# Moving the expert-weight conversion, the row scatters and the second norm's buffer inside a cross-attention + MoE kernel

## The reference, cut to what matters

```
x = x + cross_attention(layernorm(x), ctx)     # 16 batches of 256 rows of 256; 16 heads of 64; 73 + 4 keys,
                                               # two softmaxes (73 text keys, 4 image keys), low-rank
                                               # corrections on q, k, v, o
x = x + moe(layernorm(x))                      # 8 experts, top 2, 256 -> 512 (silu) -> 256
def moe(x):
    logits = x @ gate_w
    top_w  = softmax(top2(logits))
    out    = sum over the two picks of top_w * (silu(x @ w1[e]) @ w2[e])
```

## Time and profile before

| | us |
|---|---|
| median of 3 runs (829.76 to 836.23) | 834.12 |
| the profiled execution, its own time | 830.35 |
| its span in the profile | 828.6 |
| start, up to the first scores of batch 1 | 0 to 92.85 |
| batches 1 to 14, first scores to first scores | 92.85 to 528.79 |
| batch 15 and the way to the experts | 528.79 to 592 |
| experts | 592 to 828.6 |

### The profile page before, as it was taken

How to read it: one execution, slowest core, us unless ns; L and a number is a source line. 1 busy time by engine, 2 the same in 40 slices (tenths; PEclk the granted TensorE clock), 3 DMA queues, 4 the chain that set the end, 5 groups by cost and what they waited for, 6 DMA issues and landing times.

```text
span 828.6 us, 23021 instructions
## 1 busy us (share of the span) xinstructions
PE 695.4 (84%) x7980; PEld 580.9 (70%) x7981; DVE 528.4 (64%) x1226; ACT 449.2 (54%) x772; POOL 494.1 (60%) x584
## 2 busy tenths in 40 slices
PE   6757889799788789789799898864499999999994
PEld 2235777677677677677677776643398888888894
DVE  5955786686586586586586586573255555555552
ACT  1537775674675675675674675661244343443441
POOL 2227467667667667667668668666147555655565
PEclk9999999999999999999999999987599999999998
DMA  9901001101101101101101101101535556555450
GB/s 267 285 1 40 28 18 61 52 14 64 52 13 64 52 13 64 52 13 64 52 13 65 52 13 64 53 13 62 161 66 98 81 89 98 86 91 81 83 91 6
DMA packets 41676, 54.69 MB, mean 66 GB/s; under 512 B 6320, under 2 KB 36016, under 8 KB 41648
## 3 DMA queue, kind: packets, MB, share of 16 engines
q1 hardware_dynamic: 26176, 35.90, 14.8%
q0 software_dynamic: 14384, 17.33, 12.0%
q10 hardware_dynamic: 1088, 1.08, 0.4%
HBM read 30.36 MB, written 25.76 MB: 68 GB/s over the span
## 4 chain that ended last, share of the span: by engine, by line
PE 57%; ACT 14%; issue 13%; DVE 8%; DMA 2%; POOL 2%; SPq 1%; another core or an unknown queue 1%; POOLq 1%; ACTq 0%; DVEq 0%
PE ps L1321 46%; PE ps L1382 5%; ACT pt_s L873 4%; PE ps L1392 2%; ACT wstage L992 2%; ACT xn L935 2%; PE ps L439 2%; DVE ot_s L1073 2%; DMA out_x<-pt_s,token_of 1%; POOL out_x L413 1%; PE ps L1347 1%; ACT ot_s L873 1%; DVE picked L1227 1%; DVE prob L1114 1%; ACT row_words L944 1%
## 5 line engine op out<-in xcount | busy, mean ns | idle before, releaser
L413 POOL DMA_INDIRECT out_x<-pt_s,token_of x78 | 125.9, 1615 | 31.1 <-issue 30.2
L492 ACT ACTIVATE q_s<-ps 128x512 f32<-128x512 f32 x78 | 46.6, 597 | 132.6 <-PE ps L1321 132.1
L1321 PE MATMUL ps<-q_s,ffnw 128*128 128x256 f16 x936 | 110.0, 275 | 0.0
L1321 PE MATMUL ps<-ffnw,ot_s 128*128 x936 | 108.7, 273 | 0.1
L565 DVE TENSOR_TENSOR ot_s<-q_s,ot_s 128x512 f16<-128x512 f32 x78 | 54.0, 692 | 85.8 <-ACT ot_s L496 57.8
L1144 DVE TENSOR_REDUCE mx<-prob 128x16 f32<-128x1168 f32 x64 | 47.9, 790 | 95.3 <-ACT prob L913 90.9
L1321 PEld LDWEIGHTS ps<-ffnw,ot_s 128*128 128x128 f16 x936 | 90.2, 98 | 13.3 <-issue 1.9
L1321 PE MATMUL ps<-wo_s,ot_s 128*128 128x256 f16 x768 | 93.8, 281 | 5.4 <-DVE ot_s L1073 4.4
L1321 PEld LDWEIGHTS ps<-q_s,ffnw 128*128 x936 | 90.7, 99 | 10.7 <-issue 0.2
L731 POOL TENSOR_TENSOR prob<-prob,mx 128x1168 f32<-128x1168 f32 x64 | 77.6, 1235 | 31.0 <-DVE mx L1144 30.7
L1321 PE MATMUL ps<-xt_s,wq_s 128*128 128x256 f16 x768 | 89.0, 277 | 3.8 <-DVE xt_s L1073 1.9
(11 more groups left out here) (179 smaller groups left out, 1311.9 us busy)
## 6 DMA issues: line engine op xcount, KB each, us to landing
prob<-rows_dram SPq DMA_DIRECT2D x39, 264.0 KB
wstage<-in_ffn_w SPq DMA_DIRECT2D x16, 512.0 KB
x_sb<-in_x SPq DMA_DIRECT2D x4, 1024.0 KB, 11.8
out_x<-x_sb SPq DMA_DIRECT2D x16, 256.0 KB, 2.2
out_x<-pt_s,token_of POOLq DMA_INDIRECT x78
rows_dram<-wstage ACTq DMA_DIRECT2D x4, 264.0 KB
rows_dram<-wstage SPq DMA_DIRECT2D x4, 264.0 KB
pt_s<-in_wq SPq DMA_DIRECT2D x2, 512.0 KB, 4.4
```

Source lines behind the costliest of these rows:

```text
L413: pool.indirect_dma_start(out_rows, bass.IndirectOffsetOnAxis(ap=token_of[:, j % UNROLL, c:c + 1], axis=0), y_sb[:, j % UNROLL, c, :], Non ...
L492: act.activation(h32[:, half, :], h_ps(j, half), ACT.Silu, scale=1 / WSCALE).then_inc(silu_done, 1)
L1321: last = pe.matmul(o, lhs(a, n), rhs(c, n), start=(i == 0), stop=(i == len(steps) - 1))
```

## The change

Five edits. ACT's two conversions of the expert-weight piece move from behind `row_high`, near the end of a batch, to between `xt(b+1)` and `copy_scores(b, 1)` near its start. `normalise_x(b+2)` moves from between `ot` 1 and `ot` 2 to behind `exp(b, 0)`, and drops its wait for `row_lo`, since `x2n` gets a buffer of its own (2 KB per partition). ACT's `row_high(b-1)` and `gap_e(b-1)` come behind all four `ot`. DVE calls `place_rows` behind `ot` 0 and no longer behind `ot` 1, and `slot_i` is written only when the scatters that still read it are over (a new wait for `scattered`). POOL issues the four scatters one batch later, those of batch b-2, behind `normalise(b, 1)`; behind them come the weight split, `router_gap`, the bias add, `row_low` and `weigh_picks` of b-1. PE's and SP's programs stay as they are, but for the name of the buffer.

```diff
-        x2n = xn
+        x2n = sb("x2n", [P, TPB, DM], F32)
...
-            def body(b, first, last):
+                for pick in range(TOPK):
+                    for t in range(TPB):
+                        pool.indirect_dma_start(
+                            rows_dram, bass.IndirectOffsetOnAxis(ap=slot_i[:, pick, t:t + 1], axis=0),
+                            row_words[:, t, :], None).then_inc(scattered, 16)
+
+            def body(b):
+                first, settled = isinstance(b, int) and b == 0, not (isinstance(b, int) and b < 2)
                 shift(b, 0)
                 shift(b, 1)
                 normalise(b, 0)
                 if not first:
                     rstd_2(b - 1)
                 normalise(b, 1)
+                if settled:
+                    scatter(b - 2)
+                pool.wait_ge(fw_hi, b + 1)
+                fw = [ffnw[:, part, bass.ds(b, 1), :].rearrange("p e n -> p (e n)") for part in (0, 1)]
+                pool.tensor_tensor(fw[1], wstage[:], fw[0], ALU.subtract).then_inc(fw_split, 1)
                 if not first:
-                    row_low(b - 1)
+                    router_gap(b - 1)
                 pool.wait_ge(xn_done, b + 1)
...
                 if not first:
-                    router_gap(b - 1)
-                pool.wait_ge(fw_hi, b + 1)
-                fw = [ffnw[:, part, bass.ds(b, 1), :].rearrange("p e n -> p (e n)") for part in (0, 1)]
-                pool.tensor_tensor(fw[1], wstage[:], fw[0], ALU.subtract).then_inc(fw_split, 1)
-                if not first:
+                    row_low(b - 1)
                     weigh_picks(b - 1)
-                    scatter(b - 1)
-                    scatter_pick(1)
...
+            scatter(BATCH - 2)
             pool.wait_ge(fw_split, BATCH)
...
# ACT
                 if not last:
                     xt(b + 1)
+                act.wait_ge(fw_in, 16 * b + 16)
+                act.activation(wstage[:], wstage[:], ACT.Copy, scale=WSCALE).then_inc(fw_scaled, 1)
+                act.wait_ge(fw_scaled, b + 1)
+                act.activation(ffnw[:, 0, bass.ds(b, 1), :].rearrange("p e n -> p (e n)"), wstage[:], ACT.Copy
+                               ).then_inc(fw_hi, 1)
                 copy_scores(b, 1)
                 exp(b, 0)
+                if x_left:
+                    normalise_x(b + 2)
...
                 pt(b, 7)
+                for k in range(4):
+                    ot(b, k)
                 if not first:
                     row_high(b - 1)
-                act.wait_ge(fw_in, 16 * b + 16)
-                act.activation(wstage[:], wstage[:], ACT.Copy, scale=WSCALE).then_inc(fw_scaled, 1)
-                act.wait_ge(fw_scaled, b + 1)
-                act.activation(ffnw[:, 0, bass.ds(b, 1), :].rearrange("p e n -> p (e n)"), wstage[:], ACT.Copy
-                               ).then_inc(fw_hi, 1)
-                ot(b, 0)
-                ot(b, 1)
-                if not first:
                     gap_e(b - 1)
-                if x_left:
-                    act.wait_ge(row_lo, b + 1)
-                    normalise_x(b + 2)
-                ot(b, 2)
-                ot(b, 3)
...
# DVE
+                dve.wait_ge(scattered, 64 * b + 16)
                 with nc.allow_low_precision(reason="whole numbers below 2 ** 24"):
                     dve.tensor_reduce(slot_i[:].rearrange("p k t -> p (k t)"),
...
                 ot(b, 0)
-                ot(b, 1)
                 if not first:
                     place_rows(b - 1, chain)
-                ot(b, 2)
-                ot(b, 3)
+                for k in range(1, 4):
+                    ot(b, k)
```

More of the change, by code:

```diff
@@ L782, in scatter @@
                 pool.tensor_tensor(hold_p[:, 0:1], zero8[:, 0:1], zero8[:, 1:2], ALU.add)
-                scatter_pick(0)
-            def scatter_pick(pick):
-                for t in range(TPB):
-                    pool.indirect_dma_start(
-                        rows_dram, bass.IndirectOffsetOnAxis(ap=slot_i[:, pick, t:t + 1], axis=0),
-                        row_words[:, t, :], None).then_inc(scattered, 16)
-            def body(b, first, last):
+                for pick in range(TOPK):
[5 more added lines that the diff above has]
+                first, settled = isinstance(b, int) and b == 0, not (isinstance(b, int) and b < 2)
                 shift(b, 0)
@@ L804, in body @@
                 if not first:
-                    router_gap(b - 1)
-                pool.wait_ge(fw_hi, b + 1)
-                fw = [ffnw[:, part, bass.ds(b, 1), :].rearrange("p e n -> p (e n)") for part in (0, 1)]
-                pool.tensor_tensor(fw[1], wstage[:], fw[0], ALU.subtract).then_inc(fw_split, 1)
-                if not first:
+                    row_low(b - 1)
                     weigh_picks(b - 1)
-                    scatter(b - 1)
-                    scatter_pick(1)
             pool.wait_ge(misc_in, 32)
-            body(0, True, False)
-            with pool.Fori(1, BATCH - 1) as b:
-                body(b, False, False)
-            body(BATCH - 1, False, True)
+            body(0)
+            body(1)
+            with pool.Fori(2, BATCH) as b:
+                body(b)
+            scatter(BATCH - 2)
             pool.wait_ge(fw_split, BATCH)
@@ L827, in _ @@
             rstd_2(BATCH - 1)
+            router_gap(BATCH - 1)
             row_low(BATCH - 1)
-            router_gap(BATCH - 1)
             weigh_picks(BATCH - 1)
             scatter(BATCH - 1)
-            scatter_pick(1)
             ffn_pool(pool)
```

## The result

The changed kernel takes 847.85 us (median of 4 runs, 841.72 to 852.01), the kernel before 831.94 on the same chip (827.89 to 836.23): ratio 1.0192, 95% interval 1.0141 to 1.0242. It is slower by 1.9%, where 795 was forecast. The profiled execution took 852.01, its span is 850.2 (before: 828.6).

A forecast was written before the change was run, and what follows sets the result against it. PE, the busiest engine, waits 4.2 us per batch at the scores. Gains 1.98 + 1.08 - 0.1 give 2.96 per batch, 38.5 over 13; ends +1.0 and -2.0 make 790.9, plus 3.8 gives 795 us, range 782 to 815.

The forecast's parts named there:

- 1, copies leave the end: ACT's weight conversions leave the batch's end, so the next first scores start earlier: gain 1.83 us per batch.
- Part 2: Early conversions delay ACT's second score copy: cost 0.1 us per batch, bounds nothing and 2.9 with a 6.1 us load.
- 3, scatters leave the start: The four scatters no longer meet PE's second scores, whose gaps go: gain 1.98 us per batch.
- Part 4: Scatters behind the second `normalise` stall PE around `attend` 0 and 1: cost 1.0 us per batch, between 0 and 1.9.
- Part 6: POOL's split, bias add, `row_low` and `weigh_picks` behind the scatters end near t = 3.9 of the next batch: no cost.
- The clock: A lower granted clock in more batches would spoil the sum; it was left as before, with no chance given.
- The ends: Outside the steady loop: batches 0 and 1 together cost 1.0 us, the last batch and tail gain 2.0.
- Rival 3 (held signals): The moved stall also holds back PE's signals to ACT: 1.5 to 2.3 us more per batch, 815 to 825; chance 0.10.
- The slower rival: Expert piece lands late, SP waiting for POOL's split, ACT before the second copy: 860 at 5 us later; chance 0.06.
- Part 5: On DVE, `slot_i`'s new wait for scatters is free: the last leaves POOL 3.9 us before `slot_i` is due.
- The rival that ties the stall to the loop: PE's stall in the second scores stays when the scatters move: 29.16 us per batch, 811 in all; chance 0.13.
- the 2.1: In batch 0, moving the conversions away from the batch's end gives back 2.1 us.

The follow-up runs named there:

- the first experiment: The changed kernel with the four scatters, of batch b-1 again, in a row at the end of POOL's batch behind `weigh_picks`: 862.34 us, ratio 1.0304.
- the last run above: The kernel of 767.80 with its third scatter behind the second half of `normalise` and the fourth behind the weight split: 820.86 us, ratio 0.9939.
- the mended kernel: The changed kernel with paired scatters, early weight load, bias ahead of `router_gap`, batch 0's copies late, `row_high` ahead of `ot`, `row_low` behind `weigh_picks`: 777.93 us, 0.9349.
- the kernel of 767.80: The mended kernel with its four scatters one at a time, behind each half of POOL's `shift` and `normalise`: 767.80 us, ratio 0.9225.

## Why the prediction was wrong

| part | put at, us per batch | measured |
|---|---|---|
| 1, copies leave the end | -1.83 | wait for the slots -2.26 |
| 2, copies at the new place | +0.1 | +1.05 |
| 3, scatters leave the start | -1.98 | -1.98 |
| 4, scatters at the new place | +1.0 (0 to 1.9) | +2.8 |
| 6, POOL's end of batch | 0 | +0.9 |
| lower clock in batches 2 to 14 | as before | some +0.75 |
| ends: batches 0 and 1; tail | +1.0; -2.0 | +4.4; 0 |

- **Part 4 is the step that failed.** The count was near: the first gap comes 24 + 8 + 20 = 52 pairs of weight load and matmul behind the first scatter (58 counted, one or two too many, since the projection had run for 0.30 us when the first scatter began), the last one ends 5.77 us behind it (5.76). Two things were wrong. The pairs of keys and transposes run faster than I put them, and the reserve was gone after 2.5 us (378.77 - 376.24), not 3.5, so that the stall met keys and transposes and not `attend`: PE's gaps of this kind came to 0.28 + 0.46 + 0.90 = 1.64, where I had taken 1.0 (bounds 0 to 1.9). And I had put at nothing, without a reason, what the row of four does to the other engines: ACT took up late what PE had finished, so it copied keys, `pt` and `x2t` late, and PE waited 0.82 more and started each next step later. Rival 3 (held signals) said so, and the row that should have raised its chance above 0.10 was in batch 15 of the kernel before (536.86 above). Whether PE's signal comes late or ACT's own next instruction, no run here separates; ACT is late even where PE has no gap (370.14 in the first experiment). As a rival it was priced at 1.5 to 2.3 us per batch; with part 6's loss beside it that is what came.
- **Part 2.** I put the load at t = 0.2 and its landing at 3.4. SP issues the image values first, so it went out at t = 1.06 and landed at 4.8, 3.7 later. The bound of 2.9 us held. The slower rival named the right victim, ACT in front of the second copy, but the wrong culprit: SP waited for `attend`, not for POOL's split.
- **Part 6.** I weighed POOL's end of batch for when it ends, not for what runs beside it. The bias add moved beside DVE's product of the picks. The Trainium skill ("SBUF — State Buffer", section "SBUF: two separate sides") says that an operation of DVE with two SBUF inputs and a GpSimd operation that reads SBUF exclude each other. The runs agree: 1.09 and 0.97 us beside the bias add and beside `row_low`, 0.19 beside neither.
- **Part 5** was right, and what it lacked is now known in part: a single last scatter let ACT go 4.3 us after its start. If the last of a row does so too, which is an estimate, `slot_i` is free by 384.5 (380.17 + 4.3), 3.4 us before it is written (387.90).
- **Parts 1 and 3** were right. The rival that ties the stall to the loop, and with it the rule of the Trainium skill ("Runtime: NRT & Kernel Launch", "Instruction fetch mechanics") as an explanation of this stall, is refuted: the second scores are whole at the same place of the loop (1.03 us at 361.56).
- **The ends.** In batch 0 the load went out at 77.94, t = 2.9, behind the transfers of the image values. The queries came 4.5 us later, near the 5.0 I had put, but I had put nothing for the clock: the wait of 6.02 us that this makes is followed by PE at its lower level, another 2.8 us, and the 2.1 did not come back at that batch's end. With the copies late, batch 0 takes 22.4 to 22.6 in every kernel. In the tail the last projection does start 2.6 us earlier in its batch (29.55 against 32.11 after its first scores), but POOL is at the scatters of batch 14 until 588.2 and the last norm waits for it, as I had feared; the slower product takes the rest.
- **The clock.** If quiet batches are taken at 31.1 and 30.89, the lower clock has 13.3 us of the batches 2 to 14 now and had 3.6 before: some 10 of the 21.6. I had named this as the thing that could spoil the sum and given it no chance of its own. Taken over every execution that the ratios use, the spans' clocks sort the kernels only roughly: 0.926 to 0.945 with a row of four behind `normalise` and early copies (four kernels), 0.927 to 0.963 with that row and late copies (two), 0.936 to 0.956 with the row at the end of POOL's batch in the first experiment, 0.953 to 0.972 in eight kernels with pairs or single scatters, and 0.941 to 0.946 in the ninth, the last run above. With the row at its old place it is 0.967 to 0.971 with the conversions alone and 0.950 to 0.973 in the kernel before. No one wait goes with the dips: PE waits 2.26 us for the slots in the kernel before, which hardly dips, and 2.5 in that last run, which does. Why these and not others is not shown, and no run here separates it.

In all, the 61 us between the forecast span and the measured one (850.2 against 828.6 - 39.5) are 13 x 3.2 for the quiet batch, 10 for the clock, 5 at the ends and 5 at the start, to within 1 us. The 5 at the start have nothing to do with the change.

## What to carry to other kernels

Don't move a burst of indirect transfers, break it up: with a row of four the mended kernel takes 5.6% longer than with pairs and 7.0% longer than with single scatters (0.9871 against 0.9225). When a stall moves, price what its signals feed on the other engines, not only the gaps of the engine that shows it, and ask of each moved operation what will run beside it. Issue a load when its buffer is free, not when the issuing engine comes by.

## What the runs showed of the hardware

- Four scatters in a row, issued 1.3 us apart, leave PE short of instructions until 5.8 us after the first (5.76, 5.77, 5.72 in three places), and ACT takes up PE's results late in that time, by up to 2.43 us of its own idling. Two in a row leave one gap of 0.24 to 0.40 us and one late result (PE waits 0.73 to 0.87 us for ACT), single ones leave neither. A pair 2.3 us behind another is as good as one 10 us behind.
- A scatter of 128 rows holds POOL for 1.0 us and let the waiting ACT go 4.2 to 4.3 us after its start (the last kernel, three batches); in the kernel of 767.80 the same ACT instruction started 3.8 us after it without a wait.
- DVE's product of two small operands in SBUF takes 0.19 us alone and up to 1.09 beside a POOL operation of 1.2 us.
- The 512 KB load lands 3.6 us after its issue (median of 16), though its traffic before was seen to end after 3.2.
- Behind a wait of 6.02 us PE ran at its lower clock level (0.50) for 5.1 us: 12 matmuls of the queries took 2.74 us there and 1.48 at the full clock.
